# Window sums of the raw image in front of the first normalisation, its mean and factor applied afterwards, in a kernel of local attention and deformable convolution

## The reference

```python
x = x + local_attention(gn(x), W_qkv, b_qkv, W1, b1, W2, b2, Wp, bp)
x = x + deformable_conv(gn(x), w_om, b_om, w_dcn)

def gn(v):        # 32 groups of 2 channels: mean and variance over (2, 16, 16) of an image
    return (g - mean(g)) / sqrt(var(g) + 1e-5)

def local_attention(x, ...):
    y = reduce_window(x, add, 3x3, stride 1, zero padding 1) / 9     # always by 9
    q, k, v, chans = y @ W_qkv.T + b_qkv
    g = sigmoid(relu(chans @ W1.T + b1) @ W2.T + b2)
    # 8 heads; each pixel attends to its 3x3 neighbours (k and v padded with zeros)
    out = softmax(q . k_neighbours * 8 ** -0.5) . v_neighbours
    return (out * g + out) @ Wp.T + bp
```

## Time and profile before

| | us |
|---|---|
| median of 3 runs | 208.38 (208.22 to 208.55) |
| the profiled execution | 208.33 |
| its span | 206.5 |
| PE busy | 182.0 (88%) |
| DVE busy | 159.5 (77%) |
| ACT busy | 106.4 (51%) |
| POOL busy | 86.7 (42%) |

### The profile page before, as it was taken

The page is one execution under the profiler, slowest core; times in us unless marked ns, Lnnn a source line. Parts: engine busy times, 40 slices in busy tenths (PEclk is TensorE's granted clock), DMA queues, the critical chain, the costliest instruction groups (busy, mean ns, idle before and its releaser), DMA issues.

```text
span 206.5 us, 4572 instructions
## 1 busy us (share of the span) xinstructions
PE 182.0 (88%) x1808; PEld 127.9 (62%) x1808; DVE 159.5 (77%) x257; ACT 106.4 (51%) x199; POOL 86.7 (42%) x104
## 2 busy tenths in 40 slices
PE   0399996989989989999979999999969999998980
PEld 0224963644357535468668879639958789877870
DVE  0479958994869769888889779816999798899922
ACT  0325238500006795678748657836766687864000
POOL 8523982666013086504354343340561654442000
PEclk9999999999999999999999999999999999999999
DMA  6940000000040010010011000000002100000000
GB/s 193 325 28 0 3 0 2 3 0 0 0 102 14 25 30 9 17 43 3 7 29 33 0 3 0 3 0 0 12 25 62 28 0 16 2 16 2 19 0 21
DMA packets 8499, 5.54 MB, mean 27 GB/s; under 512 B 4887, under 2 KB 7461, under 8 KB 8473
## 3 DMA queue, kind: packets, MB, share of 16 engines
q1 hardware_dynamic: 8089, 4.25, 7.9%
q10 hardware_dynamic: 288, 0.89, 1.3%
q0 software_dynamic: 96, 0.06, 0.1%
HBM read 2.82 MB, written 0.52 MB: 16 GB/s over the span
## 4 chain that ended last, share of the span: by engine, by line
PE 67%; DVE 15%; ACT 6%; issue 4%; DMA 3%; POOL 2%; SPq 0%; DVEq 0%; ACTq 0%; POOLq 0%
PE ps L1218 20%; PE ps L1192 10%; PE ps L1112 10%; PE ps L1008 4%; PE ps L1129 3%; DVE smp_prod L742 3%; DMA x_parts<-in_x 3%; PE ps L1260 3%; PE ps L1266 3%; PE ps L1045 3%; PE ps L1177 2%; PE ps L991 2%; PE ps L1163 2%; DVE smp_prod L852 2%; PE ps L1146 2%
## 5 line engine op out<-in xcount | busy, mean ns | idle before, releaser
L852 DVE TENSOR_TENSOR smp_prod<-ps,hx_selx 128x768 f32<-128x768 f32 x72 | 67.5, 953 | 10.1 <-PE ps L1192 8.8
L1218 PE MATMUL ps<-smp_prod,windows_attention 128*64 128x192 f32 (+2 forms) x512 | 54.9, 336 | 0.0
L1218 PEld LDWEIGHTS ps<-smp_prod,windows_attention 128*64 128x64 f32 x512 | 40.1, 136 | 4.1 <-ACT windows_attention L574 0.3
L1192 PE MATMUL ps<-haty,by_rows 128*64 128x256 f16 x432 | 39.4, 275 | 2.0 <-DVE smp_prod L852 1.8
L450 POOL TENSOR_SCALAR disty<-disty 64x512 f32<-64x512 f32 (+1 forms) x23 | 13.5, 586 | 64.4 <-ACT haty L595 64.3
L1192 PEld LDWEIGHTS ps<-haty,by_rows 128*64 128x64 f16 x432 | 26.1, 109 | 9.7 <-DVE smp_prod L852 3.9
L603 ACT ACTIVATE hx_selx<-ps 128x512 f32<-128x512 f32 x36 | 21.3, 591 | 10.8 <-PE ps L1177 10.7
L457 POOL TENSOR_TENSOR haty<-disty,haty 64x512 f16<-64x512 f32 (+1 forms) x23 | 24.0, 1042 | 1.9
L1112 PE MATMUL ps<-conv_staged 128*108 128x512 f32 (+1 forms) x60 | 23.3, 521 | 0.7 <-ACT x_parts L567 0.7
L605 ACT ACTIVATE hx_selx<-hx_selx 128x512 f32<-128x512 f32 x36 | 22.7, 630 | 1.1
L590 ACT ACTIVATE disty<-ps 128x512 f32<-128x512 f32 (+1 forms) x24 | 12.5, 521 | 12.3 <-PE ps L1163 12.3
(11 more groups left out here) (137 smaller groups left out, 273.9 us busy)
## 6 DMA issues: line engine op xcount, KB each, us to landing
x_parts<-in_x SPq DMA_DIRECT2D x2, 256.0 KB, 5.3
bcast<-in_bcast SPq DMA_DIRECT2D x2, 256.0 KB, 6.7
x2seq<-x_parts SPq DMA_DIRECT2D x2, 256.0 KB, 3.7
out<-x_parts SPq DMA_DIRECT2D x8, 64.0 KB, 2.2
vals_attw<-in_cf ACTq DMA_DIRECT2D x1, 480.0 KB, 5.8
stack_m<-x_parts SPq DMA_DIRECT2D x12, 36.0 KB
kept<-in_cf ACTq DMA_DIRECT2D x1, 390.5 KB, 4.5
conv_staged<-in_wom SPq DMA_DIRECT2D x1, 324.0 KB, 6.9
```

Of the source, the lines that this page charges most:

```text
L852: nc.vector.tensor_tensor(pairs, rows, cols.unsqueeze(1).to_broadcast([P, QUARTERS, HW]), ALU.mult).then_inc(s_mult, 1)
L1192: ins = nc.tensor.matmul(ps[h * C:(h + 1) * C, at:at + HW], by_matrix(a, QUARTERS - 1 - k)[:, h * C:(h + 1) * C], haty[i % 2][:, p * HW:(p ...
L1218: return nc.tensor.matmul(dst[:, at:at + strips * 3 * SP].rearrange("p (s k n) -> p s k n", k=3, n=SP), rows, sampled(i, ki, m, first, str ...
```

## The change

img is gone, and with it its memset. DVE sums the windows of the raw x, in four steps a half (`window_sums`): in step 0 the last column of hsum becomes the sum of the last two of x, and each of the other 15 a pixel plus its right neighbour; step 1 adds the left neighbour to the middle 14; steps 2 and 3 add along the column as before, with hsum's zero rows above and below. A map `counts` of 9, 6 and 4 is set by four memsets. `share` is mean times rstd; `pooled_norm` makes shares = counts x share and then pooled = pooled x rstd - shares, one instruction each for every column image. The steps are put around the statistics and `norm`. On PE `keep_warm(2)` before the projections becomes `keep_warm(1)`.

```diff
-            nc.gpsimd.memset(img[:, :], 0.0).then_inc(s_zero, 1)
...
             def norm(n):
...
-                dve.wait_ge(s_rstd, n)
...
-            for j in range(J):
-                ins = normalise(shifted(img, 4)[:, j], xin, j)
-            link(ins)
...
-                link(nc.vector.tensor_tensor(mid, im[:, :, 1:H + 1, 0:W], im[:, :, 1:H + 1, 1:W + 1], ALU.add))
-                link(nc.vector.tensor_tensor(mid, mid, im[:, :, 1:H + 1, 2:W + 2], ALU.add))
-                link(nc.vector.tensor_tensor(po, hs[:, :, 0:H, :], hs[:, :, 1:H + 1, :], ALU.add))
-                nc.vector.tensor_tensor(po, po, hs[:, :, 2:H + 2, :], ALU.add).then_inc(s_pool, 1)
+            def window_sums(c, step):
+                im = halfimages(xin[:, :], c)
...
+                if step == 0:
+                    nc.vector.tensor_tensor(mid[:, :, :, W - 1:], im[:, :, :, W - 2:W - 1], im[:, :, :, W - 1:],
+                                            ALU.add).then_inc(s_counts, 1)
+                    link(nc.vector.tensor_tensor(mid[:, :, :, 0:W - 1], im[:, :, :, 0:W - 1], im[:, :, :, 1:W], ALU.add))
+                elif step == 1:
+                    link(nc.vector.tensor_tensor(mid[:, :, :, 1:W - 1], mid[:, :, :, 1:W - 1], im[:, :, :, 0:W - 2], ALU.add))
+                    dve.wait_ge(s_counts, 5 + c)
+                elif step == 2:
+                    link(nc.vector.tensor_tensor(po, hs[:, :, 0:H, :], hs[:, :, 1:H + 1, :], ALU.add))
+                else:
+                    link(nc.vector.tensor_tensor(po, po, hs[:, :, 2:H + 2, :], ALU.add))
+
+            def pooled_norm(c):
+                for j in (2 * c, 2 * c + 1):
+                    ins = nc.vector.tensor_scalar(shares[:, j * HW:(j + 1) * HW], counts, share[:, j:j + 1], None, ALU.mult)
+                link(ins)
+                for j in (2 * c, 2 * c + 1):
+                    po = pooled[:, j * HW:(j + 1) * HW]
+                    ins = nc.vector.scalar_tensor_tensor(po, po, rstd[:, j:j + 1], shares[:, j * HW:(j + 1) * HW], ALU.mult,
+                                                         ALU.subtract)
+                ins.then_inc(s_pool, 1)
+
+            dve.wait_ge(s_x[0], 16)
+            norm_stats(xin, 0)
+            dve.wait_ge(s_zero, 1)
+            window_sums(0, 0)
+            dve.wait_ge(s_x[1], 16)
+            norm_stats(xin, 2)
+            window_sums(0, 1)
+            window_sums(0, 2)
+            norm(1)
+            window_sums(0, 3)
+            window_sums(1, 0)
+            dve.wait_ge(s_rstd, 1)
+            link(nc.vector.tensor_tensor(share[:, :], pair[:, 0:2 * J].rearrange("p (j s) -> p j s", s=2)[:, :, 0], rstd[:, :],
+                                         ALU.mult))
+            pooled_norm(0)
+            for step in range(1, 4):
+                window_sums(1, step)
+            pooled_norm(1)
...
-            keep_warm(2)
+            keep_warm(1)
```

More of the change, by code:

```diff
@@ L153, in bass_local_attention_then_deformable_conv @@
         gap2 = sb("gap2", [P, J])
+        share = sb("share", [P, J])
         vareps = sb("vareps", [P, J])
@@ L176, in bass_local_attention_then_deformable_conv @@
         prod = smp[:, 0:TAPS * N]
-        ATT = [("pooled", N), ("q", N), ("chans", N), ("hidden", N), ("img", PAD), ("kpad", PAD), ("hsum", J * PH * W),
+        ATT = [("pooled", N), ("q", N), ("chans", N), ("hidden", N), ("counts", HW), ("shares", N), ("kpad", PAD), ("hsum", J * PH * W),
                ("gate", N), ("att", N), ("vpad", PAD), ("dlog", TAPS * HF), ("lmax", HF), ("den", HF)]
@@ L180, in bass_local_attention_then_deformable_conv @@
         v = views(window_words, *ATT)
-        pooled, q, chans, hidden, img, kpad, hsum, gate, att, vpad, dlog, lmax, den = (v[k] for k, _ in ATT)
+        pooled, q, chans, hidden, counts, shares, kpad, hsum, gate, att, vpad, dlog, lmax, den = (v[k] for k, _ in ATT)
         v = views(window_words, ("xs", len(PAIRROWS) * P), ("masks", 2 * MSLOT))
@@ L280, in bass_local_attention_then_deformable_conv @@
         s_stats, s_pair, s_eps, s_rstd = sem("s_stats"), sem("s_pair"), sem("s_eps"), sem("s_rstd")
+        s_counts = sem("s_counts")
         s_pool, s_qkv, s_qps, s_ev, s_chans = (sem(n) for n in ("s_pool", "s_qkv", "s_qps", "s_ev", "s_chans"))
@@ L394, in _ @@
             nc.gpsimd.memset(dup[1], 0.0).then_inc(s_zero, 1)
-            pool.wait_ge(s_zero, 7)
+            pool.wait_ge(s_zero, 6)
             pool.wait_ge(s_eps, 1)
@@ L483, in _ @@
             act.wait_ge(s_kept, 16)
-            act.wait_ge(s_zero, 5)
+            act.wait_ge(s_zero, 4)
             nc.scalar.copy(by_tap[:, :].rearrange("p (a d c) -> p a d c", a=2, d=DG),
@@ L556, in second_half @@
                 act.wait_ge(s_tall, J)
-                act.wait_ge(s_zero, 7)
+                act.wait_ge(s_zero, 6)
                 source = images(tall)[C:P, :, -FIRST_ROW * W:(-FIRST_ROW + H) * W].rearrange("p j (r c) -> p j r c", r=H)
@@ L668, in norm_stats, with norm @@
                     nc.vector.bn_aggr(meanvar[:, 2 * i:2 * i + 2], halfstat[:, 6 * i:6 * i + 6]).then_inc(s_stats, 1)
-            def norm(src, n):
+            def norm(n):
                 dve.wait_ge(s_pair, n)
@@ L685, in _ @@
             bn = [0]
[L686 to L690, removed]
-            for j in range(J):
-                ins = normalise(shifted(img, 4)[:, j], xin, j)
-            link(ins)
-            for c in range(2):
-                im = padded(img)[:, 2 * c:2 * c + 2]
+            map_ = counts.rearrange("p (r c) -> p r c", r=H)
+            for rows, cols, n in ((slice(1, H - 1), slice(1, W - 1), 9), (slice(0, H, H - 1), slice(1, W - 1), 6),
+                                  (slice(1, H - 1), slice(0, W, W - 1), 6), (slice(0, H, H - 1), slice(0, W, W - 1), 4)):
+                nc.vector.memset(map_[:, rows, cols], float(n)).then_inc(s_counts, 1)
+            def window_sums(c, step):
+                im = halfimages(xin[:, :], c)
                 hs = hsum[:, :].rearrange("p (j r c) -> p j r c", j=J, r=PH)[:, 2 * c:2 * c + 2]
@@ L780, in _ @@
                 norm_stats(x2, 2 * c)
-            norm(x2, 2)
+            norm(2)
+            dve.wait_ge(s_rstd, 2)
             low = slice(0, C)
@@ L787, in _ @@
                 normalise(shifted(dup[0], 3)[C:P, j], x2, j, low).then_inc(s_dup0, 1)
-            dve.wait_ge(s_zero, 8)
+            dve.wait_ge(s_zero, 7)
             for j in range(J):
```

## The result

| | before | changed |
|---|---|---|
| median, us | 208.39 (208.22 to 208.69, 6 runs) | 207.22 (206.66 to 207.41, 6 runs) |
| the profiled execution, its span | 208.33, 206.5 | 207.24, 205.1 |
| DVE busy | 159.5 | 161.3 |
| logits start / end of the path in front of them | 20.37 / 18.33 | 19.09 / 17.06 |

The ratio is 0.9939, 95% interval 0.9925 to 0.9952: 1.2 us faster, where 207.8 (0.53 faster) was forecast, with 206.9 to 208.8 as its range. Faster was given 0.62. The direction and the path were right; the gain was twice the forecast's, and nearly that of rival B (207.1). It lies outside the forecast's own range of 207.5 to 208.1, and inside the whole one because that was drawn around the rivals too.

What follows compares the result with a forecast made beforehand. The prediction took DVE's second-half pooling, ahead of the logits, as the bound: 1.3 us gained without hindrance, cut to 0.53 by the port, so 208.33 - 0.53 = 207.8 us. Range 206.9 to 208.8, the forecast's own 207.5 to 208.1.

Steps and rivals of the forecast that it cites:

- rival B: POOL's rstd reads and lets the SBUF port go early, so DVE isn't held: gain 1.2, 207.1 us; chance 0.24.
- The path is the second half's end: Logits wait for DVE's second-half pooling, ending at 18.33; what it gains, 0.53 us, arrives at the end undiminished.
- The first steps hide in the load, vareps comes 0.10 late: DVE's first step fits the wait for x; steps 1 and 2 delay vareps from 10.04 to 10.14.
- rstd waits for step 3: POOL's rstd stands behind DVE's two-input step 3, ending at 11.68 instead of 11.34, 1.3 to 1.4 us long.
- rstd keeps the port, S = 12.4: POOL's rstd blocks DVE's two-input sums throughout, so share starts (S) at 12.4, not 11.6; gain 0.53; chance 0.44.
- tensor_scalar at 0.407: In DVE's normalising after the sums, each 256-column tensor_scalar was priced at 0.407, giving 0.76 us a pair.
- PE does not bind: PE's first three projections end at 17.2, before the second half's pooling at 17.8, so they stay hidden.
- Rival D: TensorE's clock rises late with one warming product fewer, slow projections eat the gain: 208.7 at 18.3; chance 0.12.
- Rival E: POOL's kpad product gets between DVE's last two pooling instructions, pooling ends at 18.9, not 17.8: 208.9; chance 0.10.

Runs made afterwards that it cites:

- e4: Changed kernel with the small leftovers (own, memsets, b2half) moved from behind the pooling to right behind vareps; 207.57 us, ratio 0.9957.
- e8: As e4, plus a 512-column SBUF copy on DVE between the leftovers and step 3; one execution for its durations, 209.17 us.
- e9: Changed kernel with three extra small reductions and the leftovers in front of the second half's scalar_tensor_tensors; 212.38 us, ratio 1.0188.
- e5: Changed kernel with each half's two tensor_scalars made one of 512 columns, with two or one operands per partition; durations only, 0.55 and 0.49 us.
- the control: The changed kernel unaltered, measured once more beside some of the follow-up runs; 207.37 us, ratio 0.994 to the kernel before.
- e1: Changed kernel with both warming products, keep_warm(2) in place of keep_warm(1); 207.93 us, ratio 0.997.
- e2: Kernel before with one warming product in place of two, its DVE sums untouched; 210.60 us, ratio 1.0101.
- e3: Changed kernel with no warming product; 208.38 us, ratio 0.9986.
- e6: Changed kernel with the second half's two multiplies (counts x share) moved from DVE to ACT; 206.67 us, ratio 0.9919.
- e7: Changed kernel with the leftovers put between the second half's tensor_scalars and scalar_tensor_tensors; 207.87 us, ratio 0.9997.

## Why the prediction was right or wrong

- *The path is the second half's end.* Right. It moved from 18.33 to 17.06, the logits by 1.28, and the end by 1.2 in the medians.
- *The first steps hide in the load, vareps comes 0.10 late.* Right: 10.10 against 10.04, 0.06 late.
- *rstd waits for step 3.* Right: 1.36 long, and 1.05 once step 3 is moved (e4).
- *rstd keeps the port, S = 12.4.* Wrong, and this is the step that failed. S was 11.71, so 0.7 of the 0.8 us that the forecast took off the gain for the port (1.3 down to 0.53) was not there. The hold was weighed at 0.44 against 0.24 for B because both of its rows showed release at the recorded end. Those are instructions that pass hundreds of elements, which read until they end. rstd passes 4 elements and lasts 1.05 us. It is held up at its start by a two-input sum (1.36), and e4 and e8 show that sums and a copy run inside it at their own lengths, the first from 0.14 after its start. That it reads at once and then only computes fits all of this, but the trace doesn't show reads by themselves.
- *"SBUF — State Buffer" in the Trainium skill*, section "Who interferes with whom", has the shared port taken for the whole instruction. For wide sums and products the runs agree (e9, and cross in e4). For rstd they do not, and the measurement decides.
- *tensor_scalar at 0.407.* Wrong in the reading, and small: 0.11 a pair, of which 0.05 a pair went at the scalar_tensor_tensors and 0.06 at share. That the sum from S on held (5.34 against 5.4) is these errors cancelling. The 0.407 row was taken as the slow mode; e5 shows the fast mode plus two operands. "VectorE: DVE Perf Modes" in the Trainium skill, section "The perf-mode tier table", gives two elements a cycle for this form, and by e5 the trace agrees.
- *PE does not bind.* Right in the profile: the projections ended 0.65 before the fourth was due. But the prediction counts the dropped product only as PE being free earlier, and gives it no share in the gain. Of the 1.04 us between the control and the kernel before, e1 puts about 0.48 on the sums and 0.56 on the dropped product, and its chain shows why: with two, PE is the path. Dropped alone (e2) it costs 2.2. The two parts of the change are not additive: the drop pays only because the earlier pooling brings the projections up against the one that is left. So part of the agreement with B's 207.1 rests on a term that no sum of the prediction has.
- *Rival D* did not occur in the two profiles of the changed kernel: the clock was up at 13.1 and at about 14.2. In the six further profiles with one warming product and early pooling it rose between 12.7 and 15.6. A late rise is what happened with no product (e3, 17.3), at about the price that D had, and in the old kernel with one (e2, 19.2).
- *Rival E* did not occur, but its margin was thin. DVE's last instruction began at 16.57 and POOL's product at 16.73; POOL was the one to wait, its six took 7.21 instead of 7.02. e9 shows the price behind that margin.

## What to carry to other kernels

When an instruction moves beside another engine's, ask of each of the two how long it is likely to *read*, not how long it lasts: here a wide sum blocked its neighbour for its whole length, and a four-column power didn't measurably block it. Put the two-input instructions that end a path clearly before or behind the other engine's run of wide ones, since here (e9) two such streams took turns instruction by instruction. And look at the idle time that follows warming work: one product that led straight into the projections was enough in the changed kernel, and the same product with 1.8 us of idle behind it left the first two projections slow in the old one (e2). So try the removal of one only together with what closes the gap.

## What was not expected of the hardware

- TensorE's clock came up at about 12.7, 13.1, 13.6, 13.9, 14.2, 14.2, 15.4 and 15.6 us in the eight profiles with one warming product and early pooling (e8, changed kernel, e6, e5, the control, e4, e9, e7), at 14.8 and 14.2 with two (before, e1), at 17.3 with none (e3) and at 19.2 with one followed by 1.8 us of idle (e2). What moves the rise within a kernel stays open. The view of granted clock says 1.00 through all of it.
- Each operand per partition adds 0.058 us to a tensor_scalar at both widths (0.291, 0.350, 0.407 at 256 columns; 0.49 and 0.55 at 512). A scalar_tensor_tensor with one took 0.482, a plain two-input sum of the same width 0.426.
- A power of 4 columns on POOL takes 1.05 us and leaves DVE's reads alone; held up at its start it ends 0.9 after DVE lets go.
- Two engines that contended for the port took turns (e9). Each of DVE's two short instructions lasted about 0.95 longer for it (1.44 and 1.42 instead of 0.48), POOL's long one about 0.2 (1.38 instead of 1.17).
- The granted clock can drop for a stretch in the middle of a run (to 0.50 at 154 to 156 us in e8's profile). That execution stood 1.06 us further behind after it and 1.6 at its end. Nothing in the first stage explains it: up to 152 us the offset is constant.
